# Statistics of a normalised pair layer read seven groups ahead instead of six, a batch's mean and variance in two groups, and bias parts made later

## The chip, the cores and the metric

One core of a Trainium2 chip. The metric is the device time of one execution in microseconds. The core has five engines with instruction streams of their own: TensorE (PE; PEld are its weight loads), VectorE (DVE), ScalarE (ACT), GpSimd (POOL) and SyncE (SP), which here issues every transfer. Each runs its own stream strictly in order and waits for the others on semaphores.

## The reference

`x` has the shape 2 x 128 x 128 x 128 in f32. Two layers are added to it one after the other, each on a group-normalised copy of its input (32 groups of 4 channels). The first works on each group's rows; the second is a deformable 3 x 3 convolution with bilinear sampling.

```python
def _L0_conv_ref(pair_repr, Wa, ba, Wb, bb, Wg, bg, Wo, bo):
    a = pair_repr @ Wa + ba
    b = pair_repr @ Wb + bb
    g = jax.nn.sigmoid(pair_repr @ Wg + bg)
    ab = jnp.einsum('bijk,bikl->bijl', a, b)
    return g * ab @ Wo + bo

def _gn(v, G=32, eps=1e-05):
    g = v.reshape(B_, G, C_ // G, H_, W_)
    m = jnp.mean(g, axis=(2, 3, 4), keepdims=True)
    s = jnp.var(g, axis=(2, 3, 4), keepdims=True)
    return ((g - m) / jnp.sqrt(s + eps)).reshape(v.shape)

x = x + _L0_conv_ref(_gn(x), ...)
x = x + _L1_conv_ref(_gn(x), w_off, b_off, w_def)   # relu, offsets, bilinear gather, 3 x 3 products
```

## The kernel before, in words

Stage 1 computes the first layer, one group of 4 channels after the other, 64 groups; stage 2 computes the deformable convolution in 64 bands and starts when stage 1 has given the statistics of its result. The change and the prediction are about stage 1.

A group g is a tile of 128 rows by 4 x 128 columns. Its x is loaded by SyncE into one of XR = 8 slots, slot g % 8 (`load_x`, L466). The statistics are made for BATCH = 4 groups at a time: c is the batch, and batch c serves the groups 4c to 4c+3. The steps of group g, by engine:

- VectorE: `row_stats` (bn_stats of x, L1102) and `row_means` (L1106) run XA groups ahead, on group g + XA. Then `bm` (L1269) takes the product b out of its bank; `add_x` (L1145, L1150) adds group g-1 of the result to `x_bo` and makes its statistics; `gated` (L1294) multiplies g and ab; `x1_means` and, every fourth group, the copy L1160 keep the means.
- TensorE: the products with Wa, Wg and Wb from xT in two f16 parts (L751, L752, L756, L765, L768); `turn` (L715) transposes group g+1; `gate(g-1)` (L724) is the product with Wo; then ab (L782). L751 is the first matmul of a group.
- ScalarE: `norm_x` (L973) evicts the transposed group g+1, scaled with rstd and shifted by nbias; aT (L993); `high_x` (L982), its f16 part; gT (L999), the sigmoid.
- GpSimd: `low_x` (L1579), the rest of xT for group g+1; then `x_bo` (L1613), x of group g plus the output bias, which is the last reader of the slot of x; it waits until `add_x(g-2)` is done.
- SyncE: `load_x(g+8)`, which waits until group g has been transposed and until `x_bo(g)` is done; then `store_x1(g-1)` (L550).

In one group of four (s % 4 == 2, by `batch_ahead`, L383) the statistics of the next batch are finished. TensorE averages the row means over the partitions (`mean_sum`, L698), VectorE takes the difference from the mean and squares it (`deviations`, L1110 to L1116), TensorE averages that (`var_sum`, L705), VectorE adds up the variance (`variance`, L1121, L1126: vare), GpSimd takes the inverse root (`inverse_root`, L1567: rstd) behind `x_bo` of the group, and VectorE makes nbias (`norm_bias`, L1131). `norm_x` of the next batch waits for nbias.

The order on each engine is written out by hand in `group(g, s)` of that engine (L554, L744, L987, L1259, L1605). The first 8 and the last 8 groups are unrolled with a known g, the 48 between them run in a loop of 8. In VectorE's group before the change:

```python
if batch:
    deviations(*batch)
dve.wait_ge(b_done, g + 1)
...
if ahead:
    row_stats(g + XA, t)
if batch:
    variance(*batch)
...
if batch:
    norm_bias(*batch)
```

Before group 0 SyncE issues some 40 small transfers, then a copy of the offsets' bias (L537), six transfers of padding, and only then the load of group 8. `split_bias` on GpSimd (L1584) makes three f16 parts of that bias in five steps, one in each of the groups 0 to 4; its first step waits for the bias. In group 7 SyncE places the parts with three small transfers (L562). TensorE waits for them at the start of stage 2.

Of the kernel before, what the change touches and what calls it, by code (L numbers as in the profile page):

```python
# [9 lines left out]
GROUPS = IMGS * CH // GC  # L10
# [53 lines left out]
SUM_ROWS = BIAS_AT + BIAS_PARTS  # L64
TROWS = 3
HALF = BW // 2
CHUNK = TROWS * HALF
PIECES = 2 * TAPS // TROWS
IN_OFF = 16 * 3
IN_SELECT, SELECT_STEPS = 16 * (29 + BIAS_PARTS), 8  # L70
BIAS_STEPS = 8
BAND_STEPS, ROW_STEPS = 12, 2 + 4 * TAPS
ABG_STEPS = 11
W_STEPS = 16
# [33 lines left out]
def preact_conv_kernel(nc, x, Wa, ba, Wb, bb, Wg, bg, Wo, bo, w_off, b_off, w_def,  # L108
                       ident_d, group_mask_d, select_d, select_all_d, coords_d, out):
    with ExitStack() as ctx:  # L110
# [21 lines left out]
        XR, BATCH = 8, 4  # L132
# [30 lines left out]
        select = sb("select", [SUM_ROWS, 2, P], F16)  # L163

        BR2 = XR // BATCH
        XA = 6
        weights = sb("weights", [P, 2, 2 * TAPS, CW])
        xg = (weights[:, 1].rearrange("p k c -> p (k c)")[:, 0:XR * FG]
              .rearrange("p (s c) -> p s c", s=XR))
# [210 lines left out]
        x1_groups = x1_pad.rearrange("b (g f) r w -> (b g) r f w", f=GC)  # L380
        out_v = out.rearrange("b c h w -> b c (h w)")

        def batch_ahead(g, s):  # L383

            if s % BATCH != 2:
                return None
            if isinstance(g, int):
                c = g // BATCH + 1
                return (c, c % BR2) if c < GROUPS // BATCH else None

            return ((g - s) // BATCH + s // BATCH + 1, (s // BATCH + 1) % BR2)
# [69 lines left out]
        def _(sp):  # L461
# [92 lines left out]
            def group(g, s):  # L554
                if isinstance(g, int) and g == 5:
                    sp.wait_ge(select_set, SELECT_STEPS - 1)
                    sp.dma_start(chosen[RAW_AT:RAW_AT + NOFF], chosen[0:NOFF]
                                 ).then_inc(in_select, 16)
                if isinstance(g, int) and g == 7:
                    sp.wait_ge(bias_set, BIAS_STEPS)  # L560
                    for i in range(BIAS_PARTS):
                        sp.dma_start(select[BIAS_AT + i:BIAS_AT + i + 1],  # L562
                                     bias_parts[:, i].rearrange("p (a c) -> p a c", a=2)
                                     ).then_inc(bias_placed, 16)
                if not isinstance(g, int) or g + XR < GROUPS:
                    load_x(g + XR, s)
                if not isinstance(g, int) or g > 0:
                    store_x1(g - 1, (s - 1) % XR)
# [115 lines left out]
        def _(pe):  # L684
# [17 lines left out]
            def var_sum(c, s):  # L702

                wait(pe, dev2_ready, c + 1)
                nc.tensor.matmul(bank[B_ST][:, 2 * BATCH:3 * BATCH], average[:], dev2[:, s],  # L705
                                 start=True, stop=True).then_inc(var_summed, 1)
# [37 lines left out]
            def group(g, s):  # L744
                known = isinstance(g, int)

                pe.wait_ge(xT_hi_ready, g + 1)
                wait(pe, aT_ready, g)
                wait(pe, gT_ready, g)
                for b, j in ((B_A, 0), (B_G, 2)):  # L750
                    nc.tensor.matmul(bank[b], w_abg_hi[:, j], xT_hi[:], start=True, stop=False)  # L751
                    nc.tensor.matmul(bank[b], w_abg_lo[:, j], xT_hi[:], start=False, stop=False)  # L752
                if not known or g + 1 < GROUPS:
                    turn(g + 1, (s + 1) % XR)
                pe.wait_ge(xT_lo_ready, g + 1)
                nc.tensor.matmul(bank[B_A], w_abg_hi[:, 0], xT_lo[:], start=False,  # L756
                                 stop=True).then_inc(a_done, 1)
                wait(pe, bm_ready, g)
                if known and g == 0:
                    pe.wait_ge(rows_copied, 1)  # L760
                for f in range(GC):
                    columns = slice(f * P, (f + 1) * P)
                    for i, (part, w) in enumerate(((xT_hi, w_abg_hi), (xT_hi, w_abg_lo),
                                                   (xT_lo, w_abg_hi))):
                        mm = nc.tensor.matmul(bank[B_B][:, columns], part[:, columns], w[:, 1],  # L765
                                              start=(i == 0), stop=(i == 2))
                mm.then_inc(b_done, 1)
                nc.tensor.matmul(bank[B_G], w_abg_hi[:, 2], xT_lo[:], start=False,  # L768
                                 stop=True).then_inc(g_done, 1)
                ahead = batch_ahead(g, s)  # L770
                if ahead:
                    mean_sum(*ahead)
                if not known or g > 0:
                    gate(g - 1)
                if ahead:
                    var_sum(*ahead)
                pe.wait_ge(aT_ready, g + 1)
                pe.wait_ge(bm_ready, g + 1)
                wait(pe, gated_ready, g)
                for f in range(GC):  # L780

                    mm = nc.tensor.matmul(bank[B_AB][:, f * P:(f + 1) * P],  # L782
                                          bm[:, f * P:(f + 1) * P], aT[:, f * P:(f + 1) * P],
                                          start=True, stop=True)
                mm.then_inc(ab_done, 1)

                if known and g == 4:
                    pe.wait_ge(scaling, 4)
                    for j in (DEF, OFF):
                        mm = nc.tensor.transpose(bank[B_W][0:1, j * P:(j + 1) * P],  # L790
                                                 w_most[:, j:j + 1], ident[:])
                    mm.then_inc(scaling, 1)
                elif known and g == 6:
                    pe.wait_ge(scaling, 6)
                    nc.tensor.matmul(bank[B_W][:, 0:2], ones_row[:], w_top[:], start=True,
                                     stop=True).then_inc(scaling, 1)
# [295 lines left out]
        def _(dve):  # L1092
# [166 lines left out]
            def group(g, s):  # L1259
# [1 line left out]
                ahead = not known or g + XA < GROUPS  # L1261
                t = (s + XA) % XR
                behind = not known or g > 0
                batch = batch_ahead(g, s)
                if batch:
                    deviations(*batch)
                dve.wait_ge(b_done, g + 1)
                wait(dve, ab_done, g)
                nc.vector.scalar_tensor_tensor(  # L1269
# [13 lines left out]
                if ahead:  # L1283
                    if not behind:
                        dve.wait_ge(bn_done, g + XA + 1)
                    row_means(g + XA, t)
                if batch:
                    norm_bias(*batch)
                dve.wait_ge(ab_done, g + 1)
                dve.wait_ge(gT_ready, g + 1)  # L1290
                wait(dve, o_done, g)
                if behind:
                    dve.wait_ge(bn2_done, g)
                nc.vector.tensor_tensor(gated[:], bank[B_AB], gT[:],  # L1294
                                        ALU.mult).then_inc(gated_ready, 1)
                if behind:
                    x1_means(g - 1, (s - 1) % XR)
                    if s % BATCH == 0:
                        keep_x1_means(g - 1, (s - 1) % XR)
                if known:  # L1300
                    scale_weights(g)

# [249 lines left out]
        def _(pool):  # L1552
# [52 lines left out]
            def group(g, s):  # L1605
# [4 lines left out]
                else:  # L1610
# [4 lines left out]
                    xg[:, s, :].rearrange("p (f w) -> p f w", f=GC),  # L1615
                    all_o[:].rearrange("p (f l) -> p f l", f=1).broadcast_to([P, GC, P]),
                    ALU.add).then_inc(xbo_ready, 1)
                if batch_ahead(g, s):
                    inverse_root(*batch_ahead(g, s))

                if isinstance(g, int) and g < 5:
                    split_bias(g)
                step = g - (GROUPS - XR) if isinstance(g, int) else None
                if step == 0:
                    pool.wait_ge(scaling, 8)
# [96 lines left out]
```

## Time and profile before

| | |
|---|---|
| median of 3 runs | 1591.7 us (1590.01 to 1593.29) |
| the profiled execution | 1589.83 us, its span 1588.0 us |
| stage 1 | about 0 to 330 us |
| mean granted clock of TensorE | 0.983 |
| busy share of the span | PE 95%, PEld 63%, DVE 67%, ACT 63%, POOL 57% |

The profile shows one execution. Times are microseconds from the span's start; a duration given as a mean is in ns. A wait stands with the engine and the line that waited and those that ended the wait. The names of tiles are those of the memory they lie in: `weights` is x in its slots, `samples_hi` and `samples_lo` hold xT, aT, gT, bm, gated and x_bo in stage 1, `hy_all` holds the result on its way out; so go by the line numbers.

### The profile page before, as it was taken

What the parts mean: (1) busy time and instruction counts of PE and PEld (TensorE: products, weight loads), DVE (VectorE), ACT (ScalarE), POOL (GpSimd) and SP (SyncE); (2) the same over time, 40 slices, a digit from 0 to 9 for tenths busy, and PEclk for the clock granted to TensorE, in tenths of its full rate; (3) what the DMA queues carried; (4) which work ended last, traced back from release to release, by engine and by line L of the source; (5) the groups of instructions that cost most, each with busy time, mean ns of one, the idle gap of its engine ahead of it and who ended that gap; (6) DMA issues with size and microseconds to landing.
All of it is one profiled execution on the core that took longest, in us unless ns stands there. A gap on an engine that the chain in (4) does not pass through costs nothing.

```text
span 1588.0 us, 28169 instructions
## 1 busy us (share of the span) xinstructions
PE 1507.4 (95%) x9491; PEld 997.6 (63%) x9492; DVE 1063.6 (67%) x2154; ACT 1006.6 (63%) x1820; POOL 909.2 (57%) x563
## 2 busy tenths in 40 slices
PE   4999999956999999999999999999999999999998
PEld 3777778733666566666666666665666666666664
DVE  4888888864666666666666666666666666666664
ACT  2555555535677676667667766666677766666663
POOL 3555555725566566655566666555566665655561
PEclk9999999977999999999999999999999999999999
DMA  4333334336667666666666666766666666666550
GB/s 141 105 118 117 115 109 120 93 110 171 174 209 220 186 196 191 194 192 183 191 196 184 192 191 190 205 193 185 190 189 205 196 191 180 193 195 189 170 158 28
DMA packets 190710, 268.12 MB, mean 169 GB/s; under 512 B 19810, under 2 KB 128382, under 8 KB 190590
## 3 DMA queue, kind: packets, MB, share of 16 engines
q1 hardware_dynamic: 190590, 266.60, 57.3%
q8 instruction: 65, 1.06, 0.3%
q14 instruction: 55, 0.45, 0.1%
HBM read 188.33 MB, written 78.18 MB: 168 GB/s over the span
## 4 chain that ended last, share of the span: by engine, by line
PE 71%; issue 12%; POOL 7%; SPq 3%; DVE 3%; ACT 2%; DMA 1%; POOLq 0%; ACTq 0%; DVEq 0%
PE bank L851 31%; PE pair L816 23%; PE pair L867 7%; PE pair L896 6%; POOL samples_hi L1613 4%; DVE z_lo L1393 2%; PE pair L831 2%; PE pair L834 2%; POOL samples_lo L1579 1%; POOL rstd L1567 1%; ACT samples_hi L1071 1%; ACT abg_space L1044 1%; DMA hat_x<-hats 1%; SPq L622 1%; SPq L611 0%
## 5 line engine op out<-in xcount | busy, mean ns | idle before, releaser
L1667 POOL TENSOR_TENSOR weights<-hy_all,hx_all 112x768 f32<-112x768 f32 x384 | 723.1, 1917 | 494.2 <-PE bank L851 445.6
L1383 DVE SCALAR_TENSOR_TENSOR samples_lo<-bank,samples_hi 128x288 f16<-128x288 f32 (+1 forms) x1024 | 455.1, 464 | 335.0 <-ACT samples_hi L1071 327.2
L1071 ACT ACTIVATE samples_hi<-bank 128x288 f16<-128x288 f32 (+1 forms) x1024 | 402.9, 421 | 313.5 <-PE bank L851 293.0
L851 PE MATMUL bank<-weights,zT 112*128 112x288 f32 (+1 forms) x2176 | 596.8, 403 | 0.0
L851 PEld LDWEIGHTS bank<-weights,zT 112*128 112x128 f32 x2176 | 380.5, 190 | 131.4 <-issue 36.4
L816 PE MATMUL pair<-samples_hi,w_hi 128*128 128x512 f16 x576 | 218.7, 380 | 1.3 <-DVE samples_lo L1383 1.3
L816 PE MATMUL pair<-samples_lo,w_hi 128*128 128x512 f16 x576 | 217.5, 378 | 0.0
L816 PE MATMUL pair<-samples_hi,w_lo 128*128 128x512 f16 x576 | 217.3, 377 | 0.0
L867 PE MATMUL pair<-ident,z 128*112 128x128 f32 x1088 | 172.4, 273 | 8.3 <-DVE zT L1403 7.1
L867 PEld LDWEIGHTS pair<-ident,z 128*112 128x112 f32 x1088 | 133.0, 134 | 64.8 <-DVE zT L1403 8.3
L973 ACT ACTIVATE samples_hi<-pair,nbias,rstd 128x512 f32<-128x512 f32 x64 | 49.8, 777 | 153.9 <-PE pair L715 98.3
L1579 POOL TENSOR_TENSOR samples_lo<-samples_hi,samples_lo 128x512 f16<-128x512 f32 x64 | 74.1, 1158 | 124.9 <-ACT samples_lo L982 124.8
L1021 ACT ACTIVATE z<-raw,norm_band 128x1904 f32<-128x1904 f32 (+3 forms) x80 | 130.9, 1656 | 0.0
L1081 ACT COPY zT<-pair 112x512 f32<-112x512 f32 (+1 forms) x192 | 92.2, 480 | 35.3 <-PE pair L867 31.5
L1044 ACT ACTIVATE abg_space<-raw,norm_band 128x660 f32<-128x660 f32 (+2 forms) x74 | 104.1, 1420 | 11.9 <-DMA raw<-x_pad 11.9
L896 PE MATMUL pair<-z_hi,woff 128*32 128x512 f16 x1152 | 90.4, 410 | 12.7 <-ACT z_hi L1032 12.7
L816 PEld LDWEIGHTS pair<-samples_lo,w_hi 128*128 128x128 f16 x576 | 55.2, 96 | 69.3
L1368 DVE TENSOR_SCALAR hats<-dist 128x1024 f32<-128x1024 f32 x64 | 45.3, 708 | 78.3 <-ACT dist L1064 70.2
L1403 DVE COPY zT<-pair 112x512 f32<-112x512 f32 x128 | 87.8, 686 | 11.6 <-PE pair L867 11.6
L816 PEld LDWEIGHTS pair<-samples_hi,w_lo 128*128 128x128 f16 x576 | 56.5, 98 | 59.9
L816 PEld LDWEIGHTS pair<-samples_hi,w_hi 128*128 128x128 f16 x576 | 55.8, 97 | 59.6 <-DVE samples_lo L1383 18.0
L1064 ACT ACTIVATE dist<-pair 128x1024 f32<-128x1024 f32 x64 | 65.6, 1025 | 38.1 <-PE pair L834 38.1
(141 smaller groups left out, 1772.7 us busy)
## 6 DMA issues: line engine op xcount, KB each, us to landing
hy_all<-hat_y SPq DMA_DIRECT2D x384, 192.0 KB
hx_all<-hat_x SPq DMA_DIRECT2D x384, 192.0 KB
hat_y<-hats SPq DMA_DIRECT2D x256, 126.0 KB
raw<-x_pad SPq DMA_DIRECT2D x68, 272.0 KB, 4.3
x_pad<-hy_all SPq DMA_DIRECT2D x64, 272.0 KB, 3.4
weights<-in_x SPq DMA_DIRECT2D x64, 256.0 KB, 3.0
out<-y SPq DMA_DIRECT2D x32, 512.0 KB, 3.6
hat_x<-hats SPq DMA_DIRECT2D x128, 72.0 KB
```

The lines of the kernel that those rows point to most:

```text
L816: mm = nc.tensor.matmul(bank[B_CONV].rearrange("p (h c) -> p h c", h=2), w_part[:, k, :], part[:, u, k::TAPS, k % 3 * HR:k % 3 * HR + HALF ...
L851: mm = nc.tensor.matmul(sampled_step(n, p)[:, :, c0 - first:c1 - first], zT[0:WPIX, u * WINDOWS + w, :], weights[0:WPIX, u, :, c0:c1], sta ...
L867: mm = nc.tensor.transpose(bank[B_ZT][0:WPIX, (w % 4) * P:(w % 4 + 1) * P], z[:, u, w].rearrange("p r c -> p (r c)"), ident[:])
L896: mm = nc.tensor.matmul(bank[B_OFF][at:at + 32, :].rearrange("p (w r) -> p w r", r=BR), w[:, k, :], pixels[:, kx:kx + UW, ky:ky + BR], sta ...
L1021: done = nc.scalar.activation(z[:, u, :, rows, :], patches, ACT.Relu, bias=norm_band[:, 1].rearrange("p b n -> p (b n)")[:, n:n + 1], scal ...
L1044: done = nc.scalar.activation(z_near[:, :, r0:r1], raw[:, src:src + r1 - r0, left:left + UW + 2].rearrange("p r w -> p w r"), ACT.Relu, bi ...
L1071: nc.scalar.activation(samples_hi[:, u, :, c0:c1], sampled_step(n, p), ACT.Copy).then_inc(samples_ready, 1)
L1081: nc.scalar.copy(zT[0:WPIX, at:at + c, :].rearrange("p w c -> p (w c)"), bank[B_ZT][0:WPIX, 0:c * P]).then_inc(zT_a, 1)
L1383: nc.vector.scalar_tensor_tensor(out=samples_lo[:, u, :, c0:c1], in0=sampled_step(n, p), scalar=1.0, in1=samples_hi[:, u, :, c0:c1], op0=A ...
L1403: nc.vector.tensor_copy(zT[0:WPIX, at:at + c, :].rearrange("p w c -> p (w c)"), bank[B_ZT][0:WPIX, 0:c * P]).then_inc(zT_v, 1)
L1579: nc.gpsimd.tensor_tensor(xT_lo[:], xT[:], xT_hi[:], ALU.subtract).then_inc(xT_lo_ready, 1)
L1667: nc.gpsimd.tensor_tensor(to, hy_all[0:WPIX, i * TROWS:(i + 1) * TROWS, :], hx_all[0:WPIX, i * TROWS:(i + 1) * TROWS, :], ALU.mult).then_i ...
```

## The change

The row statistics run seven groups ahead instead of six (XA). `batch_ahead` gets the place in the batch as an argument: the mean's matmul stands in groups with s % 4 == 1 ahead of `gate`, and VectorE's `deviations` at the end of that group; the variance's matmul stands in the next group, ahead of `gate` too, and `norm_bias` behind `gated`. The five steps of `split_bias` move from groups 0 to 4 to groups 3 to 7, and the three transfers of its parts from group 7 to group 56.

```diff
--- before.py
+++ after.py
@@ -64,11 +64,12 @@
 SUM_ROWS = BIAS_AT + BIAS_PARTS
 TROWS = 3
 HALF = BW // 2
+MEAN_AT, VAR_AT = 1, 2
 CHUNK = TROWS * HALF
 PIECES = 2 * TAPS // TROWS
 IN_OFF = 16 * 3
 IN_SELECT, SELECT_STEPS = 16 * (29 + BIAS_PARTS), 8
-BIAS_STEPS = 8
+BIAS_STEPS, BIAS_SPLITS = 8, 5
 BAND_STEPS, ROW_STEPS = 12, 2 + 4 * TAPS
 ABG_STEPS = 11
 W_STEPS = 16
@@ -163,7 +164,7 @@
         select = sb("select", [SUM_ROWS, 2, P], F16)
 
         BR2 = XR // BATCH
-        XA = 6
+        XA = 7
         weights = sb("weights", [P, 2, 2 * TAPS, CW])
         xg = (weights[:, 1].rearrange("p k c -> p (k c)")[:, 0:XR * FG]
               .rearrange("p (s c) -> p s c", s=XR))
@@ -380,9 +381,9 @@
         x1_groups = x1_pad.rearrange("b (g f) r w -> (b g) r f w", f=GC)
         out_v = out.rearrange("b c h w -> b c (h w)")
 
-        def batch_ahead(g, s):
-
-            if s % BATCH != 2:
+        def batch_ahead(g, s, at):
+
+            if s % BATCH != at:
                 return None
             if isinstance(g, int):
                 c = g // BATCH + 1
@@ -556,7 +557,7 @@
                     sp.wait_ge(select_set, SELECT_STEPS - 1)
                     sp.dma_start(chosen[RAW_AT:RAW_AT + NOFF], chosen[0:NOFF]
                                  ).then_inc(in_select, 16)
-                if isinstance(g, int) and g == 7:
+                if isinstance(g, int) and g == GROUPS - XR:
                     sp.wait_ge(bias_set, BIAS_STEPS)
                     for i in range(BIAS_PARTS):
                         sp.dma_start(select[BIAS_AT + i:BIAS_AT + i + 1],
@@ -767,13 +768,12 @@
                 mm.then_inc(b_done, 1)
                 nc.tensor.matmul(bank[B_G], w_abg_hi[:, 2], xT_lo[:], start=False,
                                  stop=True).then_inc(g_done, 1)
-                ahead = batch_ahead(g, s)
-                if ahead:
-                    mean_sum(*ahead)
+                if batch_ahead(g, s, MEAN_AT):
+                    mean_sum(*batch_ahead(g, s, MEAN_AT))
+                if batch_ahead(g, s, VAR_AT):
+                    var_sum(*batch_ahead(g, s, VAR_AT))
                 if not known or g > 0:
                     gate(g - 1)
-                if ahead:
-                    var_sum(*ahead)
                 pe.wait_ge(aT_ready, g + 1)
                 pe.wait_ge(bm_ready, g + 1)
                 wait(pe, gated_ready, g)
@@ -1261,9 +1261,7 @@
                 ahead = not known or g + XA < GROUPS
                 t = (s + XA) % XR
                 behind = not known or g > 0
-                batch = batch_ahead(g, s)
-                if batch:
-                    deviations(*batch)
+                batch = batch_ahead(g, s, VAR_AT)
                 dve.wait_ge(b_done, g + 1)
                 wait(dve, ab_done, g)
                 nc.vector.scalar_tensor_tensor(
@@ -1284,8 +1282,6 @@
                     if not behind:
                         dve.wait_ge(bn_done, g + XA + 1)
                     row_means(g + XA, t)
-                if batch:
-                    norm_bias(*batch)
                 dve.wait_ge(ab_done, g + 1)
                 dve.wait_ge(gT_ready, g + 1)
                 wait(dve, o_done, g)
@@ -1293,10 +1289,14 @@
                     dve.wait_ge(bn2_done, g)
                 nc.vector.tensor_tensor(gated[:], bank[B_AB], gT[:],
                                         ALU.mult).then_inc(gated_ready, 1)
+                if batch:
+                    norm_bias(*batch)
                 if behind:
                     x1_means(g - 1, (s - 1) % XR)
                     if s % BATCH == 0:
                         keep_x1_means(g - 1, (s - 1) % XR)
+                if batch_ahead(g, s, MEAN_AT):
+                    deviations(*batch_ahead(g, s, MEAN_AT))
                 if known:
                     scale_weights(g)
 
@@ -1615,11 +1615,11 @@
                     xg[:, s, :].rearrange("p (f w) -> p f w", f=GC),
                     all_o[:].rearrange("p (f l) -> p f l", f=1).broadcast_to([P, GC, P]),
                     ALU.add).then_inc(xbo_ready, 1)
-                if batch_ahead(g, s):
-                    inverse_root(*batch_ahead(g, s))
-
-                if isinstance(g, int) and g < 5:
-                    split_bias(g)
+                if batch_ahead(g, s, VAR_AT):
+                    inverse_root(*batch_ahead(g, s, VAR_AT))
+
+                if isinstance(g, int) and XR - BIAS_SPLITS <= g < XR:
+                    split_bias(g - (XR - BIAS_SPLITS))
                 step = g - (GROUPS - XR) if isinstance(g, int) else None
                 if step == 0:
                     pool.wait_ge(scaling, 8)
```

## Rows read from the trace of the kernel before

**Rows 1.** Head of the page: the span of the profiled execution.

```profile
span 1588.0 us, 28169 instructions
```

**Rows 2.** Busy time in the stretch of groups 34 to 37; columns in its first line.

```profile
core 0: us, PE busy (x) PEld busy (x) DVE busy (x) ACT busy (x) POOL busy (x), PEclk, DMA share, GB/s
187.80:206.60 18.80, 17.95 (x158) 14.92 (x158) 16.18 (x36) 10.54 (x16) 10.68 (x10) 1.00 0.37 113
```

**Rows 3.** Waits from 60 to 310 us: total, times, longest.

```profile
ACT samples_hi L973 <- DVE nbias L1131: 45.9, 14, 4.0
...
SPq L92 <- POOL samples_hi L1613: 170.6, 50, 4.8
```

**Rows 4.** Line 466, the loads of x, from 60 to 290 us: landing.

```profile
DMA to landing us min/median/max: 2.8/3.0/3.1
```

**Rows 5.** Order of time, plain groups: start, us, engine, line, operation, out<-in.

```profile
182.18 0.69 DVE L1102 BATCH_NORM_STATS2 st<-weights 128x6 f32<-128x512 f32 x1
...
183.51 0.38 PE L751 MATMUL pair<-samples_lo,abg_space 128*128 128x512 f16 x1
...
184.56 0.69 DVE L1294 TENSOR_TENSOR samples_hi<-bank,samples_hi 128x512 f32<-128x512 f32 x1
...
185.39 0.38 SPq L466 DMA_DIRECT2D weights<-in_x  x1
185.48 0.17 DVE L1160 COPY mv<-mv 128x8 f32 x1
...
185.91 1.05 PE L724 MATMUL bank<-w_o,samples_hi 128*128 128x128 f32 x8
...
186.56 0.68 DVE L1102 BATCH_NORM_STATS2 st<-weights 128x6 f32<-128x512 f32 x1
...
186.80 1.08 PE L782 MATMUL bank<-samples_hi 128*128 128x128 f32 x8
...
187.79 0.38 PE L751 MATMUL pair<-samples_lo,abg_space 128*128 128x512 f16 x1
...
188.15 1.30 POOL L1613 TENSOR_TENSOR samples_hi<-weights,all_o 128x512 f32<-128x512 f32 x1
...
206.57 0.38 PE L751 MATMUL pair<-samples_lo,abg_space 128*128 128x512 f16 x1
```

**Rows 6.** Order of time in groups 34 and 35; last line: all of L1126, ns.

```profile
191.08 0.75 DVE L1269 SCALAR_TENSOR_TENSOR samples_hi<-pair,abg_unscale,all_b 128x512 f32<-128x512 f32 x1
...
191.93 1.13 PE L782 MATMUL bank<-samples_hi 128*128 128x128 f32 x8 [0.35 <-issue]
...
192.43 1.29 POOL L1613 TENSOR_TENSOR samples_hi<-weights,all_o 128x512 f32<-128x512 f32 x1
...
193.83 1.02 POOL L1567 TENSOR_TENSOR rstd<-vare,minus_half 128x4 f32<-128x4 f32 x1
...
195.07 0.13 DVE L1131 SCALAR_TENSOR_TENSOR nbias<-mg,rstd 128x4 f32<-128x4 f32 x1
...
195.23 0.78 ACT L973 ACTIVATE samples_hi<-pair,nbias,rstd 128x512 f32<-128x512 f32 x1 [3.31 <-DVE nbias L1131]
...
196.57 0.61 ACT L982 CAST samples_lo<-samples_hi 128x512 f16<-128x512 f32 x1
...
198.38 1.31 POOL L1613 TENSOR_TENSOR samples_hi<-weights,all_o 128x512 f32<-128x512 f32 x1
...
199.91 0.39 SPq L466 DMA_DIRECT2D weights<-in_x  x1
...
L1126 DVE TENSOR_SCALAR vare<-spread x16: 170/1204/1297, 10.3 to 304.9; 128x4 f32<-128x4 f32 x16
```

**Rows 7.** Order of time at the start, 30 to 42 us.

```profile
33.95 1.14 POOL L1579 TENSOR_TENSOR samples_lo<-samples_hi,samples_lo 128x512 f16<-128x512 f32 x1
...
35.09 1.69 SPq L466 DMA_DIRECT2D weights<-in_x  x2
...
39.68 1.83 PE L782 MATMUL bank<-samples_hi 128*128 128x128 f32 x8
...
41.34 0.38 PE L751 MATMUL pair<-samples_lo,abg_space 128*128 128x512 f16 x1
```

## The prediction

> **What bounds the kernel now.** I read the page first, then the busy time by stretch, the waits, and the order of time in the stage that the change touches. The profiled execution spans 1588.0 us [rows 1] and took 1589.83 us with what lies around the span; the median of the runs, 1591.7 us, stands 1.9 us above it. All edits lie in stage 1, the 64 groups of the first 330 us; what follows starts when stage 1 is done, so a microsecond there is a microsecond of the total.
>
> In stage 1 TensorE is nearly the bound. A stretch of four groups, 18.80 us, has it busy for 17.95 us at granted clock 1.00 [rows 2]. A plain group takes 4.28 us: the one that starts at 183.51 is followed by the next at 187.79 [rows 5]. But from the first matmul of group 34 (187.79) to that of group 38 (206.57) pass 18.78 us [rows 5], where four plain groups would take 17.12. The difference, 1.66 us, is the price of a batch's statistics, two small matmuls and two waits: ScalarE waited 45.9 us in 14 places for nbias [rows 3], and TensorE behind it. That is what the new order of mean, variance and nbias attacks, at most 1.66 x 15 = 25 us.
>
> The other thing to see is where the loads of x start. The transfer queue waited 170.6 us in 50 places for GpSimd's x_bo [rows 3]: load_x(g+8) goes out only when x_bo(g) has read the slot. A load lands 3.0 us (2.8 to 3.1) after its issue [rows 4].
>
> **The change, part by part.**
>
> *Statistics seven groups ahead.* With XA = 6, row_stats in group g reads the slot that x_bo(g-2) freed; with XA = 7 it reads that of x_bo(g-1), a whole group younger. In the group that starts at 183.51 (group 33), load_x(40) is issued at 185.39 and lands at 188.4, while VectorE reaches row_stats at 186.56 [rows 4, 5]. Today that instruction takes x(39), loaded long ago; after the change it takes x(40), which is 1.8 us away. VectorE runs in order, so behind the wait stand add_x(g-1), the second statistics and gated(g); TensorE's gate(g) and AB(g+1), ScalarE's gT(g+1) and the store of x1 wait for those. This is a new wait, and it closes a loop: first matmul, turn, norm_x, low_x, x_bo, load, row_stats, gated, TensorE again.
>
> *Its price.* The longest loop runs over one batch, from the first matmul of group 4i+2 to that of group 4i+6, and each piece has its row:
> - first matmul to x_bo: 183.51 to 188.15, 4.64 us [rows 5];
> - x_bo to rstd, which follows it on GpSimd: 192.43 to 193.83, 1.40; rstd itself 1.02 [rows 6];
> - nbias to norm_x: 195.07 to 195.23, 0.16 [rows 6];
> - norm_x through high_x and low_x to x_bo of group 4i+3: 195.23 to 198.38, 3.15 [rows 6];
> - that x_bo to the load's issue: 198.38 to 199.91, 1.53 [rows 6], and landing 3.0 [rows 4];
> - row_stats of group 4i+4 through add_x, gated and the means to the copy of the means: 182.18 to 185.48, 3.30, and the copy's own 0.17 [rows 5];
> - bm of group 4i+5 to AB: 191.08 to 191.93, 0.85 [rows 6]; AB to the next group's first matmul: 186.80 to 187.79, 0.99 [rows 5].
>
> Sum: 4.64 + 1.40 + 1.02 + 0.16 + 3.15 + 1.53 + 3.00 + 3.30 + 0.17 + 0.85 + 0.99 = 20.21 us, against 18.78 today: 1.43 us more in each batch. From group 6 to group 58 there are 13 batches; the last of these statistics are made in group 56, so behind that nothing changes. 13 x 1.43 = 18.6 us. Hand-overs that overlap by some tenths, and a landing of 2.8, would make the loop 19.9: +14 us. The lower end is the loop without the batch's own steps, which runs over three plain groups: 4.64 + 1.53 + 3.00, row_stats to gated 2.38 (182.18 to 184.56), gated itself 0.69, and gate to the next first matmul 1.88 (185.91 to 187.79), 14.1 us in three groups or 18.8 in four [rows 4, 5, 6]: no change.
>
> The Trainium skill (DMA: Bandwidth & Descriptors, "Anatomy of one DMA") puts a transfer at about 2.0 us fixed plus its bytes over 436 GB/s, which for a 256 KB load is an estimate of 2.6 us. That formula is given there for transfers issued from GpSimd; by it the loop would be 0.4 us shorter in each batch and the total some 5 us lower. The trace's 3.0 decides.
>
> *Mean in group 4i+1, variance in 4i+2.* The three little operations and the wait for the mean leave the front of bm; that is the gain counted above, and the loop swallows it, because bm now waits behind the late statistics instead. The mean's matmul needs the row means of group g+6, which now come from VectorE's group just before: it stands ahead of gate on TensorE and may wait there, but gate waits for the same VectorE's gated, which comes later. nbias moves behind gated (0.69 us [rows 5]); in the loop rstd is about as late, so it costs nothing or 0.1 to 0.2 us.
>
> *vare beside x_bo.* The scaling of the variance takes 0.17 us or up to 1.3 us (median 1.20) [rows 6]: the long ones begin while x_bo runs on GpSimd and end with it. In the loop rstd follows that same x_bo on GpSimd, so a long vare delays only add_x of that group, which is off the loop: 0, at most 1.1 us in a batch.
>
> *The bias parts.* split_bias(0) leaves group 0, where GpSimd waits for the bias transfer and so starts the low_x of group 2 only at 33.95 [rows 7]; by its place in a plain group (1.1 us ahead of x_bo) it was due before 29. Alone that would give back some 5 us. But the loads of x(8) and x(9) are issued only at 35.09, behind the same small transfers [rows 7], and x(8) is now wanted in group 1 instead of group 2. It lands at about 38.1; add_x(0), the statistics and gated(1) then end near 41, and gate(1), AB(2) and the first matmul of group 3 come at the low clock that the trace shows after such a stop (AB 1.83 us at 39.68 against 1.08 at 186.80 [rows 5, 7]): group 3 near 45.6 instead of 41.34 [rows 7]. Start: +4.3 us, with ends of 0 and +6. The five small steps in groups 3 to 7 find GpSimd idle between x_bo's end and the next low_x, 10.68 us busy in 18.80 [rows 2]: nothing. The three transfers of the parts move from group 7 to group 56, where no load is left to be held up; TensorE wants them at the end of stage 1: nothing, and without that cover three issues of 0.38 us, as a load's [rows 5].
>
> Sum: 18.6 + 4.3 = +22.9 us: 1612.7 for a profiled execution, 1614.6 for the median.
>
> **The rivals.**
> 1. *The late load binds* (forecast): 1614.6, between 1604 and 1623. Chance 0.77.
> 2. *Faster: the loads come in time.* It decides if x(g+7) lands before VectorE reaches it, which needs the load 1.8 us earlier than in rows 4 and 5. Then rstd binds: first matmul to norm_x is 4.64 + 1.40 + 1.02 + 0.16 = 7.2 us, high_x ends 1.95 later (195.23 to 196.57, and its 0.61 [rows 6]), at 9.2 where two plain groups take 8.56, so a batch takes 17.12 + 0.6 and some 0.3 for its two small matmuls, 18.0: 13 x 0.7 = 9 us less, 1583. For it speaks only that no row shows this wait yet; against it the issue at 185.39 [rows 5]. Chance 0.07.
> 3. *The two cancel.* The loop is no longer than a batch today (18.8 by the plain loop) and the start's two stops trade places: 1590 to 1595. Chance 0.05.
> 4. *Landing grows.* Loads now land while VectorE waits; at 3.5 us instead of 3.0 the loop gains another 0.5 x 13 = 6.5 us, and long vares on the path 0.3 a batch: 1621 to 1626. Chance 0.08.
> 5. *TensorE's clock falls in every batch.* After the stop at the start [rows 7] the products took 1.83 us instead of 1.08 [rows 5]; the new gaps are below 1 us each, and today's gaps, 0.85 us in a batch, leave the clock at 1.00 [rows 2]. A fall that lasts one group (4.28 us, longer by 0.7) costs 3 us; in 15 batches 45 us: 1660 (an estimate from these rows). [...] Chance 0.03.
>
> **How the numbers follow.** A measurement of this kernel tells about 0.2% (3.2 us) from no change. Faster holds rival 2, 0.07; same is rival 3, 0.05; slower the rest, 0.88. The range takes the loop from 19.9 to 20.7 us a batch and the start from -2 to +6: 1604 to 1623, which leaves out rivals 2, 3, 5 and half of 4.
>
> **What would show it.** In the profile after: waits of VectorE's first statistics (bn_stats of x) for the load, in about two of four groups, 1 to 2 us each; batches of about 20.2 us instead of 18.78; ScalarE's wait for nbias still there; GpSimd's low_x no longer waiting for the bias transfer at 33 us but VectorE waiting for x(8) until 38. If VectorE shows no wait for a load in steady groups, the forecast's first step is wrong; if it does and the batch still takes 18.8 or less, the loop was put together wrongly.

## The result, and the profile after

The changed kernel takes 1628.15 us (median of 4 runs, 1626.65 to 1628.63) against 1592.2 us before (4 runs beside it): ratio 1.022, interval 1.0207 to 1.0233. It is slower, as forecast, but by 36 us instead of 23, outside the range of 1604 to 1623.

Head of the page of the kernel after:

```profile
span 1626.3 us, 28174 instructions
```

The span has grown by 38.3 us [rows 1]. Where, can be read from the first matmul of single groups (L751 before, L752 after) in the order of time:

| first matmul of | before, us | after, us | later by |
|---|---|---|---|
| group 3 | 41.34 | 45.87 | 4.5 |
| group 6 | 56.15 | 62.02 | 5.9 |
| group 10 | 75.11 | 83.37 | 8.3 |
| group 58 | 300.53 | 335.41 | 34.9 |
| group 63 | 324.69 | 360.67 | 36.0 |
| end of the span | 1588.0 | 1626.3 | 38.3 |

So the loss lies in stage 1 and grows nearly evenly in its loop. From here on "a batch" is the time from group 10 to group 58 over 12: 18.78 us before, 21.00 after. (What is left of the span behind group 63 was between 1262.4 and 1265.6 us in all kernels of this study, without a pattern; the last 2.3 us of the table are of that kind.)

The waits from 60 to 340 us of the kernel after (total, times, longest):

```profile
ACT samples_hi L973 <- DVE nbias L1131: 39.7, 13, 3.5
DVE st L1102 <- DMA weights<-in_x: 38.2, 26, 2.0
```

The second line has no counterpart in [rows 3]: VectorE's bn_stats of x now wait for a load, 26 times in 52 groups, 1.5 us in the mean. The wait for nbias is still there, 3.1 us a time in the mean (45.9 us in 14 places, 3.3 a time, before [rows 3]).

Order of time of the kernel after, one turn of the loop, from the first matmul of group 26 to that of group 30:

```profile
168.01 0.38 PE L752 MATMUL pair<-samples_lo,abg_space 128*128 128x512 f16 x1
...
172.66 1.29 POOL L1613 TENSOR_TENSOR samples_hi<-weights,all_o 128x512 f32<-128x512 f32 x1
...
173.92 1.01 POOL L1567 TENSOR_TENSOR rstd<-vare,minus_half 128x4 f32<-128x4 f32 x1
...
175.17 0.78 ACT L973 ACTIVATE samples_hi<-pair,nbias,rstd 128x512 f32<-128x512 f32 x1 [3.02 <-DVE nbias L1131]
...
178.31 1.28 POOL L1613 TENSOR_TENSOR samples_hi<-weights,all_o 128x512 f32<-128x512 f32 x1
...
179.82 0.38 SPq L467 DMA_DIRECT2D weights<-in_x  x1
...
182.97 0.69 DVE L1102 BATCH_NORM_STATS2 st<-weights 128x6 f32<-128x512 f32 x1 [1.89 <-DMA weights<-in_x]
...
185.75 1.16 POOL L1579 TENSOR_TENSOR samples_lo<-samples_hi,samples_lo 128x512 f16<-128x512 f32 x1 [1.89 <-ACT samples_lo L982]
...
186.16 0.78 DVE L1160 COPY mv<-mv 128x8 f32 x1
186.85 0.74 DVE L1267 SCALAR_TENSOR_TENSOR samples_hi<-pair,abg_unscale,all_b 128x512 f32<-128x512 f32 x1
...
187.69 1.13 PE L782 MATMUL bank<-samples_hi 128*128 128x128 f32 x8 [0.53 <-issue]
...
188.66 0.38 PE L752 MATMUL pair<-samples_lo,abg_space 128*128 128x512 f16 x1
```

This is the loop of the prediction, and up to the statistics its steps are within 0.15 us of the sum: x_bo to rstd takes 1.26 us (1.40 there), and from the load's issue to the statistics pass 3.15 (3.00); the others differ by less. From the late statistics (182.97) through add_x and gated to the copy of the means (186.16) pass 3.19 us; [rows 5] gave 3.30. But the copy itself lasts 0.78 us where it had 0.17 [rows 5]. It begins while GpSimd's low_x runs (185.75 to 186.91) and ends with it, and bm and everything behind it start that much later. Before, GpSimd was idle by then:

```profile
182.76 1.16 POOL L1579 TENSOR_TENSOR samples_lo<-samples_hi,samples_lo 128x512 f16<-128x512 f32 x1 [2.08 <-ACT samples_lo L982]
183.87 1.30 POOL L1613 TENSOR_TENSOR samples_hi<-weights,all_o 128x512 f32<-128x512 f32 x1
```

low_x ended at 183.92 and x_bo at 185.17, and the copy began at 185.48 [rows 5]. All copies of the kernel after, ns (min/median/max), and then all of the kernel before:

```profile
L1160 DVE COPY mv<-mv x16: 172/813/1125, 58.1 to 369.0; 128x8 f32 x12, 128x8 f32<-128x8 f32 x4
```

```profile
L1160 DVE COPY mv<-mv x16: 171/172/173, 53.2 to 333.0; 128x8 f32 x12, 128x8 f32<-128x8 f32 x4
```

In the kernel after, 13 of the 16 begin beside low_x, from 80 to 333 us; each of them ends 0.03 us after it.

Two stretches are slower still. Windows of the kernel after (columns as in [rows 2]), first an undisturbed batch, then the two:

```profile
188.66:209.50 20.84, 18.77 (x158) 14.99 (x156) 16.53 (x36) 10.64 (x16) 10.58 (x9) 1.00 0.34 104
123.50:130.90 7.40, 7.01 (x48) 5.80 (x49) 5.46 (x14) 2.64 (x4) 1.69 (x2) 0.77 0.24 74
270.00:278.00 8.00, 7.54 (x52) 6.01 (x51) 6.06 (x15) 2.64 (x4) 2.30 (x3) 0.79 0.25 75
```

and the order of time at the first of them, with AB (L782) two batches later behind it:

```profile
123.89 1.68 PE L782 MATMUL bank<-samples_hi 128*128 128x128 f32 x8 [0.69 <-issue]
125.36 0.63 PE L752 MATMUL pair<-samples_lo,abg_space 128*128 128x512 f16 x1
...
167.04 1.13 PE L782 MATMUL bank<-samples_hi 128*128 128x128 f32 x8 [0.71 <-issue]
```

The granted clock 0.77 is a mix of the two levels, 2.4 GHz and 1.2 GHz. TensorE had idled for 0.69 us ahead of AB, which then took 1.68 us where it takes 1.08 at full clock [rows 5]; the matmul behind it took 0.63 instead of 0.38. The batches 104.02 to 125.36 to 147.16 take 21.34 + 21.80 us, 250.99 to 272.12 to 294.12 take 21.13 + 22.00; beside twice 20.74 (the undisturbed 20.84 and, from 209.50 to 230.14, 20.64) each fall costs 1.7 us. A third stretch of this kind lies behind group 58, from 345.0 to 350.7 us (granted clock 0.70).

### The profile page after: what moved, and what is told of

The parts are those of the page before. It is cut to its first block, busy times and chain, and to the rows that moved or that the text cites. A ratio compares the mean times of both kernels' runs of the same rounds, so it can differ in the third digit from the quotient of the medians.

```text
span 1626.3 us, 28174 instructions
## 1 busy us (share of the span) xinstructions
PE 1522.4 (94%) x9491; PEld 1002.7 (62%) x9492; DVE 1069.9 (66%) x2154; ACT 1008.2 (62%) x1820; POOL 909.3 (56%) x563
## 4 chain that ended last, share of the span: by engine, by line
PE 70%; issue 14%; POOL 6%; SPq 4%; DVE 3%; ACT 2%; DMA 1%; POOLq 0%; ACTq 0%; DVEq 0%
PE bank L851 30%; PE pair L816 22%; PE pair L867 7%; PE pair L896 6%; POOL samples_hi L1613 4%; PE pair L831 2%; PE pair L834 2%; DVE z_lo L1393 2%; POOL rstd L1567 1%; DMA hat_x<-hats 1%; POOL samples_lo L1579 1%; ACT samples_hi L1071 1%; ACT abg_space L1044 1%; SPq L623 1%; SPq L612 0%
## 5 line engine op out<-in xcount | busy, mean ns | idle before, releaser
L782 PE MATMUL bank<-samples_hi 128*128 128x128 f32 x512 | 72.8, 286 | 20.6 <-issue 10.5
```

## The experiments

The theory of the forecast was: the late load makes a loop, the loop sets the batch. What was open after the result is why the loop is 0.8 us longer than its sum, whether the other edits do anything, and whether any of the gain that the new order was after is there. Ratios are to the kernel before, with their intervals; "the new order" is the mean in one group and the variance in the next.

**Seven ahead alone.** The kernel before, with one edit:

```diff
-        XA = 6
+        XA = 7
```

> The kernel before with XA = 7 and nothing else. Theory (the load that row_stats now needs is issued too late, because x_bo of the group just before must free its slot): VectorE waits for loads of x in steady groups as after the change, a batch of four groups takes 20 to 21 us instead of 18.8, and the time is 1615 to 1630 us. Rival (the new order of mean, variance and nbias, or the later bias parts, is what costs): within 5 us of the kernel before, 1588 to 1597 us.

Measured: 1629.15 us, ratio 1.0238 (1.0216 to 1.026), a batch 21.43 us, a little more than was expected. Its wait from 60 to 330 us, and its copies:

```profile
DVE st L1102 <- DMA weights<-in_x: 24.0, 22, 2.0
```

```profile
L1160 DVE COPY mv<-mv x16: 170/882/1070, 58.0 to 371.9; 128x8 f32 x12, 128x8 f32<-128x8 f32 x4
```

This one number carries the whole loss; the order and the bias parts are not its cause. The batch is 0.4 us longer than in the change, 0.14 of it by a third fall of the clock in the loop. That the other edits help a little in this loop would fit that, but the two times are not told apart.

**The copy without its wait.** The changed kernel, with the copy of the means written as a maximum over one element each, which gives the same values:

```diff
-                nc.vector.tensor_copy(
+                nc.vector.tensor_reduce(
...
-                    mv1[:, s // BATCH].rearrange("p g k -> p (g k)")).then_inc(mv2_ready, BATCH)
+                    mv1[:, s // BATCH].rearrange("p g (k o) -> p (g k) o", o=1), AX.X,
+                    ALU.max).then_inc(mv2_ready, BATCH)
```

> The changed kernel with the copy of four groups' means (0.81 us in the median, 0.17 before the change) made as a reduction over one element. Theory (the copy waits for GpSimd's low_x and lies in the loop of the late load): the operation takes under 0.3 us, each batch loses 0.6 us, 13 batches 8 us: 1618 to 1623 us. Rival (the copy is off the loop): within 2 us of the changed kernel, 1626 to 1630 us.

Measured: 1614.83 us, ratio 1.0147 (1.0131 to 1.0163): 13.3 us less than the change. A batch takes 20.09 us instead of 21.00. The same line in this kernel, and one turn of it in order of time:

```profile
L1160 DVE TENSOR_REDUCE mv<-mv x16: 160/160/164, 58.4 to 356.2; 128x8 f32 x12, 128x8 f32<-128x8 f32 x4
```

```profile
180.90 1.16 POOL L1580 TENSOR_TENSOR samples_lo<-samples_hi,samples_lo 128x512 f16<-128x512 f32 x1 [1.88 <-ACT samples_lo L982]
...
181.28 0.16 DVE L1160 TENSOR_REDUCE mv<-mv 128x8 f32 x1
```

It still begins in the middle of low_x (180.90 to 182.06), and no longer waits for its end. Group 63 starts at 347.90 instead of 360.67, 12.8 us earlier. Of that, 11.0 us lie between group 10 and group 58: 0.65 us in each of 12 batches (20.74 less 20.09) are 7.8, and the two falls of the clock are 3.3; this kernel shows no fall ahead of group 63. The expectation had left the falls out, so the time came out below it. That the falls went because the batch got shorter is not shown. The batch is now within 0.12 us of the sum of 20.21 us that the prediction made.

The Trainium skill (SBUF — State Buffer, "Who interferes with whom") says that VectorE's copies and casts in their fast form and GpSimd exclude each other from a shared port pair, and that tensor_reduce never contends for it. These rows agree with both halves; in which form this copy ran, no run here shows.

**The bias parts alone, and taken out again.** On the kernel before, the five steps in groups 3 to 7 and the three transfers in group 56; on the changed kernel, both back where they were. Of the first edit, the steps:

```diff
...
-                if isinstance(g, int) and g < 5:
-                    split_bias(g)
+                if isinstance(g, int) and XR - BIAS_SPLITS <= g < XR:
+                    split_bias(g - (XR - BIAS_SPLITS))
```

> The kernel before with the bias parts made in groups 3 to 7 and placed in group 56, nothing else. By the prediction's part on its own: 5 us less, 1587 us. Rival (x(8), which row_stats wants in group 2 and which is issued only at 35 us, is the next stop): the first matmul of group 3 comes early, near 31 us, the stop moves into group 3, and group 4 starts within 1.5 us of before; 1590 to 1593 us.

Measured: 1590.64 us, ratio 0.9995 (0.9986 to 1.0004). Group 3 starts at 32.60 instead of 41.34, group 4 at 45.07 instead of 46.13. Between them, in order of time:

```profile
34.98 0.99 SPq L466 DMA_DIRECT2D weights<-in_x  x2
...
38.04 0.69 DVE L1102 BATCH_NORM_STATS2 st<-weights 128x6 f32<-128x512 f32 x1 [6.50 <-DMA weights<-in_x]
```

Of the 8.7 us that group 3 wins, 7.7 are lost again one group later: x(8) is loaded only behind the small transfers, and VectorE's row statistics in group 2 want it. Two stops lay one behind the other, and the first had hidden the second.

> The changed kernel with the bias parts made in groups 0 to 4 again and placed in group 7. Theory (the wait for x(8) in group 1 hides the wait for the bias transfer): group 3 starts within 1 us of the changed kernel's 45.9 us, and the time is within 3 us, 1625 to 1631 us. Rival (the later bias parts save the stop that the prediction named): 5 us more, 1633 us.

Measured: 1623.66 us, ratio 1.0202 (1.0185 to 1.0219), 4.5 us less than the change and 1.3 below the expectation; the intervals overlap. Group 3 starts at 45.75 (45.87 in the change): the start does not see the bias parts. Stage 1 is 1.4 us shorter, with one fall of the clock in the loop instead of two; the rest is behind group 63, within the spread told above. That the bias parts cost something in the change is not shown, and they gain nothing in it either.

**The root ahead of x_bo.** The kernel with the reduced copy, and GpSimd's `inverse_root` moved in front of `x_bo` in groups with s % 4 == 2. By the prediction's loop that takes x_bo's 1.3 us out of it:

```diff
+                if batch_ahead(g, s, VAR_AT):
+                    inverse_root(*batch_ahead(g, s, VAR_AT))
...
-                if batch_ahead(g, s, VAR_AT):
-                    inverse_root(*batch_ahead(g, s, VAR_AT))
```

> The changed kernel with 8 slots, the copy as a reduction, and rstd on GpSimd ahead of x_bo of its group instead of behind it. Theory (the loop runs over x_bo and rstd of group 4i+2, as summed in the prediction): 1.2 to 1.3 us less in each of 13 batches, so a batch of 18.8 to 19.1 us and 1599 to 1604 us. Rival (rstd is off the loop; only the loads of plain groups count): 1612 to 1617 us, as with the copy alone.

Measured: 1622.18 us, ratio 1.0184 (1.0166 to 1.0203): 7 us more than without the edit and above both expectations, a batch 20.77 us. Waits from 60 to 300 us (without the edit the first is 35.0 us in 30 places, and the second is not there), and then the order of time in one such group:

```profile
DVE st L1102 <- DMA weights<-in_x: 47.7, 34, 2.6
POOL rstd L1568 <- DVE vare L1126: 8.1, 11, 2.2
```

```profile
172.02 1.02 POOL L1568 TENSOR_TENSOR rstd<-vare,minus_half 128x4 f32<-128x4 f32 x1 [0.57 <-DVE vare L1126]
173.01 1.29 POOL L1616 TENSOR_TENSOR samples_hi<-weights,all_o 128x512 f32<-128x512 f32 x1
...
174.53 0.38 SPq L467 DMA_DIRECT2D weights<-in_x  x1
...
177.38 0.69 DVE L1102 BATCH_NORM_STATS2 st<-weights 128x6 f32<-128x512 f32 x1 [2.30 <-DMA weights<-in_x]
```

x_bo of that group now stands behind rstd, which waits for vare, which stands behind the late statistics; so its own load goes out later, and the next statistics wait 2.3 us. Read so, the loop of the prediction is one of several that are nearly as long, and what shortens it lengthens another; no run here tests that reading by itself.

**The late statistics last.** The changed kernel with VectorE's `row_stats` moved behind everything else of its group (`row_means` follows behind bm of the next group), so that nothing of this group is queued behind the wait:

```diff
...
-                if ahead:
-                    row_stats(g + XA, t)
+                if made:
+                    row_means(g - 1 + XA, (s - 1 + XA) % XR)
...
+                if ahead:
+                    row_stats(g + XA, t)
...
```

> The changed kernel, 8 slots, with row_stats of group g+7 last in VectorE's group instead of ahead of add_x and gated, and row_means behind bm of the next group. Theory (the load is late only because VectorE asks for it too early in its group: it lands 1.8 us behind its place, and the end of the group is about 3 us behind that place): most of the wait for loads goes, and with it most of the loss; a batch of 18.8 to 19.4 us, 1596 to 1608 us. Rival (the load is late by more than the group's rest, or the wait only moves into bm): within 5 us of the changed kernel, 1623 us or more.

Measured: 1608.74 us, ratio 1.0107 (1.009 to 1.0124), a batch 19.93 us. The statistics of all 52 groups from 60 to 340 us (busy us, mean ns, idle before them), the waits from 60 to 330 us, and the copies of the means:

```profile
L1102 DVE BATCH_NORM_STATS2 st<-weights 128x6 f32<-128x512 f32 x52 | 35.1, 675 | 0.0
```

```profile
DVE hy_all L1145 <- PE bank L725: 24.5, 27, 1.6
PE bank L699 <- DVE mv L1106: 12.6, 13, 1.0
```

```profile
L1160 DVE COPY mv<-mv x16: 171/172/184, 54.2 to 351.2; 128x8 f32 x12, 128x8 f32<-128x8 f32 x4
```

No statistics wait for a load any more, and a little more than half of the 36 us come back. What is late in their place is the means: TensorE waits for them ahead of the mean's matmul (12.6 us; 5.5 in the change), gate stands behind that, and VectorE's add_x waits for gate (24.5 us; 0.3 in the change). The time came out 0.7 us above the expectation, the batch 0.5. But what came back is not all the work of the statistics' new place. The copies of the means no longer fall beside low_x in this order and take 0.17 us, as the reduced copy did above (0.16); and group 3 starts at 41.65 instead of 45.87. Beside the kernel with the reduced copy, a batch is 0.16 us shorter (19.93 against 20.09) and the start 4.1 us. In the loop the new place by itself wins little: both places for the late statistics have somebody behind them.

**Twelve slots.** The changed kernel with four more slots for x, so that load_x(g+12) goes out behind x_bo(g) and seven ahead reads what was freed five groups ago (the bias parts then lie in groups 7 to 11 and their transfers in group 52, by their own formulas); and the kernel before with the same edit:

```diff
-        XR, BATCH = 8, 4
+        XR, BATCH = 12, 4
...
-        xg = (weights[:, 1].rearrange("p k c -> p (k c)")[:, 0:XR * FG]
+        xg = (weights[:].rearrange("p u k c -> p (u k c)")[:, 4 * TAPS * CW - XR * FG:]
...
```

What is left out at its end counts the loads that a wait for x asks for, by the new number of slots.

> The changed kernel with 12 slots for x instead of 8, so that a load is issued five groups ahead of its statistics. Theory: no wait of VectorE for a load in steady groups, a batch takes 18.2 to 18.8 us, and the stop at the start shrinks since x(8) is loaded early; 1578 to 1592 us. Rival (the new order costs by itself): a batch stays at 20 us or more, 1612 us or more.

Measured: 1580.54 us, ratio 0.9928 (0.9911 to 0.9945). No wait for a load is left in the loop. One batch of it:

```profile
115.05:133.63 18.58, 17.91 (x157) 14.83 (x157) 15.82 (x36) 10.53 (x16) 10.52 (x10) 1.00 0.41 119
```

Group 3 starts at 32.59, group 10 at 67.24 instead of 75.11, group 63 at 315.71 instead of 324.69. So 7.9 of the 9.0 us that stage 1 wins are won before group 10. (From group 10 to group 58 a batch takes 18.81 us, about what it took before. But with twelve slots the extra steps that stand in the last XR groups begin in group 52, and the batch from group 54 on takes 20.0 us. So kernels with twelve slots are compared from group 14 to group 50.) Whether fewer than twelve slots would do was not run.

> The kernel before (six ahead, old order) with 12 slots for x. Tells how much of the 1580.5 us of the changed kernel with 12 slots comes from the slots and how much from the new order. Theory: its loads were never late in steady groups, so a batch stays at 18.8 us; the start keeps its stop for the bias transfer, some 2 us later than now because four more loads go out first: 1590 to 1596 us. Rival (the slots alone bring the gain): 1579 to 1584 us.

Measured: 1593.34 us, ratio 1.0003 (0.9993 to 1.0013). The slots alone give nothing: group 3 starts at 44.00, held by the bias as before (GpSimd waits 11.2 us for its transfer).

**Twelve slots and the bias parts, in the old order.** Which edit of the change earns its part of the 11 us that the change gains with twelve slots (1580.54 against 1591.91 beside it)? The kernel before with twelve slots and the late bias parts (the edits above), statistics six ahead, mean and variance in one group:

> The kernel before with twelve slots and the bias parts made later (groups 7 to 11, as in the changed kernel with twelve slots), but statistics six ahead and mean and variance in one group as before. Theory (the start gives most of what twelve slots gain with the change; the order of mean and variance gives 0.2 us a batch): neither stop of the start is left, so group 3 begins near 32.6 and group 10 near 67 instead of 75.1, and a batch stays at 18.8: 1592 - 8 = 1584, between 1582 and 1586. Rival (the gain needs the new order: with the old one the start catches on the next stop): group 10 near 75 to 79, 1590 to 1594. Rival 2 (the order gives nothing at all and all 11 us come from slots and bias): 1580.

Measured: 1581.56 us, ratio 0.9937 (0.992 to 0.9953), 0.4 us under the range of the theory and 1.6 above the second rival. Group 10 starts at 68.75, group 63 at 317.46; from group 14 to group 50 a batch takes 18.68 us, with the new order 18.63, before 18.79. This kernel and the one with the whole change differ by 1.0 us, and the intervals overlap, so theory and second rival are not told apart: the new order and the seventh group are worth little or nothing. The gain is that of the start, where both stops have to go: the bias parts take away the first, the slots the second, and each alone gives nothing.

**The wait for nbias.** With the change and twelve slots ScalarE still waits 40.5 us in 13 places for nbias. Twelve slots, the reduced copy and the root ahead of x_bo together:

> The changed kernel with 12 slots, rstd ahead of x_bo and the copy as a reduction: no late load, and nbias earlier by x_bo's 1.3 us. Theory (with the loads in time, nbias is what is left of a batch's price): a batch of 17.4 to 18.0 us instead of 18.6, 8 to 14 us off 1580.5: 1566 to 1573 us. Rival (another wait takes its place): 1577 to 1582 us.

Measured: 1579.09 us, ratio 0.9909 (0.9889 to 0.9929); far above what the theory expected, and against twelve slots alone inside the intervals; from group 14 to group 50 a batch takes 18.61 us, with twelve slots alone 18.63. In the window of that kernel above, TensorE is busy for 17.91 of 18.58 us, so waits could give back at most 0.67 us a batch. In order of time nbias had not gained:

```profile
166.17 1.27 POOL L1616 TENSOR_TENSOR samples_hi<-weights,all_o 128x512 f32<-128x512 f32 x1
...
166.56 0.69 DVE L1291 TENSOR_TENSOR samples_hi<-bank,samples_hi 128x512 f32<-128x512 f32 x1
167.16 0.30 DVE L1131 SCALAR_TENSOR_TENSOR nbias<-mg,rstd 128x4 f32<-128x4 f32 x1
```

rstd is done when x_bo begins behind it, at 166.17, but VectorE begins gated at 166.56, and nbias stands behind that. So, on top, nbias ahead of gated:

```diff
+                if batch:
+                    norm_bias(*batch)
...
-                if batch:
-                    norm_bias(*batch)
```

> The changed kernel with 12 slots, rstd ahead of x_bo and the copy as a reduction (1579.1 us), and nbias ahead of gated, where it stood before the change. Theory (nbias stands 0.7 us behind its input because gated is ahead of it): 0.5 to 0.7 us less in each of 13 batches, 1570 to 1573 us. Rival (gated now waits for rstd instead): 1577 to 1581 us.

Measured: 1580.21 us, ratio 0.9927 (0.9911 to 0.9944): nothing. In order of time, and then all of them in the loop (busy us, mean ns):

```profile
185.75 1.27 POOL L1616 TENSOR_TENSOR samples_hi<-weights,all_o 128x512 f32<-128x512 f32 x1
...
186.00 1.03 DVE L1131 SCALAR_TENSOR_TENSOR nbias<-mg,rstd 128x4 f32<-128x4 f32 x1
186.96 0.68 DVE L1293 TENSOR_TENSOR samples_hi<-bank,samples_hi 128x512 f32<-128x512 f32 x1
```

```profile
L1131 DVE SCALAR_TENSOR_TENSOR nbias<-mg,rstd 128x4 f32<-128x4 f32 x13 | 13.6, 1046 | 0.6 <-POOL rstd L1568 0.6
```

Now nbias falls beside x_bo, lasts 1.03 us instead of 0.13 [rows 6] and ends with it. gated stands behind nbias, and TensorE's gate waits for gated. From 60 to 340 us this wait is as follows; in the kernel without this last edit it was 1.4 us, once:

```profile
PE bank L725 <- DVE samples_hi L1293: 10.4, 13, 1.4
```

A version of this order with eight slots was not tried, nor nbias on another engine.

## Why the prediction was right and wrong

**The first step was right.** The load of x(g+7) lands after VectorE reaches it; it was to happen in about two of four groups at 1 to 2 us, and it happened 26 times in 52 with 2.0 us at most. Undone (twelve slots), the whole loss is gone; done alone (seven ahead), the whole loss is there.

**The start was right.** Group 3 was put near 45.6 us and came at 45.87:

```profile
35.21 0.99 SPq L467 DMA_DIRECT2D weights<-in_x  x2
...
38.37 0.69 DVE L1102 BATCH_NORM_STATS2 st<-weights 128x6 f32<-128x512 f32 x1 [11.44 <-DMA weights<-in_x]
```

The 4.3 us were 4.5. What stood beside it, that the bias parts "alone would give back some 5 us", was wrong: alone they give nothing, since the wait for x(8) was next in line. The same rows from which the 4.3 us were worked out said so. (The range of the prediction takes the start from -2, its own part on the start from 0; the miss does not hang on that.)

**The loop was put together rightly, and one of its terms was mis-sized.** The step that failed is "the copy's own 0.17". The sum of 20.21 us is within 0.12 of what the kernel with the reduced copy does (20.09), and in the turn shown above every other step is within 0.15 us of its row, some longer and some shorter. Beside low_x the 13 copies of the changed kernel take 0.85 us in the mean, and with the copy as it is the batch takes 0.65 us more: 20.74 in the undisturbed batches. The duration was taken from a row in which the copy lay clear of GpSimd's work. In the loop, VectorE's group is late against GpSimd's and the copy falls into low_x. For vare the prediction had read just this, that an operation which begins beside GpSimd's work ends with it [rows 6]; it did not ask the same of the other small operations in the loop after moving them in time.

At group 63 the whole reads so: 36.0 us later, where the sum of the prediction was 22.9. The start is 4.5 of it (4.3 in the sum). The 13 batches from group 6 to group 58 are 29.0 (18.6 in the sum); of the 10.4 beyond the sum, 6.9 are 13 times 0.53 us (20.74 less 20.21) and 3.3 the two falls of the clock. Groups 3 to 6 are 1.3 and groups 58 to 63 are 1.1, both put at nothing. The 1.1 go with the third fall: from group 58 to group 63 pass 25.3 us in the change, and 24.2 before and with the reduced copy, where it is not there. The 1.3 are not explained.

**The clock was a smaller miss.** Two falls in the loop at 1.7 us are another 0.28 us a batch: 20.09 + 0.65 + 0.28 = 21.0, as measured. Neither the rival with a fall in every batch nor the forecast with none was right, and a fall costs 1.7 us instead of the 3 that the rival put it at. What decides whether a gap makes the clock fall stays open: ahead of AB a gap of 0.69 us preceded one fall and one of 0.46 us the other (at 270.65), while gaps of 0.53 us (at 187.69) and 0.71 us (at 167.04) passed without one.

**The other rivals.** Loads in time (1583) and the two cancelling (1590 to 1595) are excluded by the waits. Twelve slots put the loads in time, and 1580.54 us is near that 1583; but by chance: the rival had a batch of 18.0 us, which takes 18.63, and 7.9 us come from the start, where it had nothing. Landing did not grow: 2.7/2.9/3.7 us (min/median/max) against [rows 4]; the long vares did not lie on the way.

**The gain that the loop was said to swallow** was put at up to 25 us. [rows 2] already left less: TensorE was busy for 17.95 of 18.80 us, so waits could give back at most 0.85 us a batch, 13 us in 15. With the loop gone it is 0.16 us a batch against before (from group 14 to group 50), and not told apart from nothing against the kernel with the old order. ScalarE waits for nbias nearly as long as before (with twelve slots 40.5 us in 13 places, 3.1 a time; 3.3 in [rows 3]): rstd behind x_bo, and nbias behind gated or beside x_bo, hold what the earlier mean wins. How much of that wait could still be won is open; the two attempts at it gave nothing.

## What to carry to other kernels

When a step is read further ahead, count the groups between the release of its buffer and the read, and check that load, landing and the work before it fit in there; if they don't, the buffer's depth has to grow with the distance. When a step moves in time, its duration moves too: take it from a row in which the other engines do what they will do beside it, or bound it by one. And before a stop at the start is removed, look for the next stop behind it; two in a row have to go together.

## What the hardware showed unexpectedly

A copy of 128 x 8 values on VectorE takes 0.17 us alone and up to 1.13 us in the changed kernel beside GpSimd's two-input operations on 128 x 512; the same values moved by a tensor_reduce take 0.16 us in either place. A two-input operation on 128 x 4 values (nbias) went from 0.13 to 1.05 us in the mean in the same way. In these rows the wait is as long as what is left of GpSimd's instruction, however small the one that waits is.
